# Re-ordering the first sixty microseconds of a cross-attention and quantized feed-forward kernel: weight sums shared anew, first layers moved ahead of side products

## The reference, cut to what matters

```
x = x + cross_attention(layernorm(x), ctx)         # x: 4 x 2048 x 512, ctx: 4 x 154 x 512
x = x + ffn(layernorm(x))

# the mask lets query i see key j only where j % 2048 == i, so that a row
# with i < 154 gets (ctx[i] @ Wv) @ Wout + bout, and every other row the mean of these
def qlinear(x, w, b):
    xq = clip(round(x * sx)), sx = 127 / max|x| of the row
    wq = clip(round(w * sw), -1, 1), sw = 1 / mean|w| of the whole weight
    return (xq @ wq.T) / (sx * sw) + b
h   = layernorm(x) * gamma + beta
h   = gelu(qlinear(h, w1, b1))                       # 512 -> 2048
out = qlinear(h, w2, b2)                             # 2048 -> 512
```

## Time and profile before

| | |
|---|---|
| median of 3 runs | 541.45 us (538.63 to 542.35) |
| the profiled execution | 540.51 us, of which the span is 538.7 us |
| busy in the span | PE 98%, DVE 84%, ACT 81%, POOL 76% |
| the chain of work that ended last | PE 95%, DVE 3%, POOL 1%, ACT 1% |
| stretch from the first to the second weight use (34.15 to 80.81 us) | PE 39.6 of 46.7 us busy, DVE 41.2, ACT 41.1, POOL 37.7 |

### The profile page before, as it was taken

One profiled execution on the slowest core, in us unless ns is written; L12 is line 12 of the kernel. 1 busy time (PEld: TensorE's weight loads), 2 busy tenths in 40 slices (PEclk: granted clock), 3 DMA queues, 4 the chain that ended last, 5 costly groups with the idle time before them and its releaser, 6 DMA issues.

```text
span 538.7 us, 8129 instructions
## 1 busy us (share of the span) xinstructions
PE 527.3 (98%) x2434; PEld 227.4 (42%) x2434; DVE 453.6 (84%) x758; ACT 435.9 (81%) x444; POOL 407.3 (76%) x533
## 2 busy tenths in 40 slices
PE   9979989999999999999999999999999999999997
PEld 5433434444444444444444444444444444444443
DVE  3877999999989899988888887988888889887653
ACT  3558899888887888888888888888888889887762
POOL 2288687999998888888888988888888888873300
PEclk9987999999999999999999999999999999999999
DMA  8999233886565656555665556665455574535433
GB/s 310 402 387 294 69 69 102 170 208 162 135 122 141 131 148 119 129 125 130 131 143 142 123 129 117 141 132 132 124 123 130 129 142 103 92 86 100 95 78 98
DMA packets 137015, 78.72 MB, mean 146 GB/s; under 512 B 114246, under 2 KB 114310, under 8 KB 136972
## 3 DMA queue, kind: packets, MB, share of 16 engines
q1 hardware_dynamic: 135636, 75.80, 57.3%
q10 hardware_dynamic: 1335, 2.41, 1.3%
HBM read 33.88 MB, written 17.05 MB: 95 GB/s over the span
## 4 chain that ended last, share of the span: by engine, by line
PE 95%; DVE 3%; POOL 1%; ACT 1%; issue 1%; POOLq 0%; DVEq 0%; ACTq 0%
PE py L1055 41%; PE p L1040 28%; PE pab L1040 14%; PE p L983 3%; PE p L1030 3%; PE pab L1008 2%; PE pab L1030 1%; POOL xr L387 1%; PE pab L968 1%; DVE hx L792 1%; PE py L1016 1%; PE py L1008 1%; DVE w2q L779 1%; ACT hid L578 0%; PE py L974 0%
## 5 line engine op out<-in xcount | busy, mean ns | idle before, releaser
L1055 PE MATMUL py<-w2q,hqT 128*128 128x512 bf16 x1024 | 231.0, 379 | 1.7 <-DVE hqT L829 1.7
L587 ACT ACTIVATE hq<-hid,hscale 128x2048 int8<-128x2048 f32 x64 | 128.1, 2002 | 46.2 <-DVE hscale L821 46.2
L1040 PE MATMUL p<-w1q,xqT 128*128 128x512 bf16 x688 | 159.4, 380 | 0.0
L1055 PEld LDWEIGHTS py<-w2q,hqT 128*128 128x128 bf16 x1024 | 100.1, 98 | 123.0 <-DVE hqT L829 2.7
L578 ACT ACTIVATE hid<-p,xdeq 128x1024 f32<-128x1024 f32 x86 | 95.0, 1106 | 15.9 <-PE p L1040 11.2
L1040 PEld LDWEIGHTS p<-w1q,xqT 128*128 128x128 bf16 x688 | 63.8, 98 | 81.2 <-issue 10.1
L387 POOL TENSOR_TENSOR xr<-xr,attn 128x512 f32<-128x512 f32 x64 | 83.3, 1320 | 18.7 <-DVE attn L727 17.2
L402 POOL TENSOR_TENSOR hx<-hx,beta_b 128x512 f32<-128x512 f32 x64 | 91.7, 1454 | 4.4 <-ACT hx L563 4.3
L815 DVE TENSOR_REDUCE hmax<-hid 128x1 f32<-128x1025 f32 x64 | 78.1, 1220 | 18.0 <-ACT hid L578 17.4
L406 POOL TENSOR_TENSOR xr<-xr,b_b 128x512 f32<-128x512 f32 x64 | 92.6, 1465 | 0.0
L809 DVE TENSOR_REDUCE hid<-hid 128x1 f32<-128x1024 f32 x64 | 77.4, 1209 | 8.8 <-ACT hid L578 8.8
(11 more groups left out here) (88 smaller groups left out, 408.9 us busy)
## 6 DMA issues: line engine op xcount, KB each, us to landing
xr<-x SPq DMA_DIRECT2D x64, 256.0 KB, 2.9
out<-xr SPq DMA_DIRECT2D x64, 256.0 KB, 2.4
raw<-w1T SPq DMA_DIRECT2D x8, 512.0 KB, 12.2
hid<-wvT SPq DMA_DIRECT2D x8, 256.0 KB, 7.8
wout<-wout_d ACTq DMA_DIRECT2D x8, 256.0 KB, 8.7
wout<-w2T SPq DMA_DIRECT2D x3, 512.0 KB, 5.5
xr<-w2T SPq DMA_DIRECT2D x2, 512.0 KB, 11.1
attn<-ctxm_d SPq DMA_DIRECT2D x4, 256.0 KB, 8.1
```

Source lines behind the costliest of these rows:

```text
L587: nc.scalar.activation(hq8[:, t % 2, :], hid[:, t % 2, 0:HID], ACT.Copy, scale=col(hscale, t))\
L1040: mm = nc.tensor.matmul(hidden_bank(t, n), xT[:, k, :], w1q[:, k, n * D:(n + 1) * D], start=False, stop=(k == KD - 1))
L1055: mm = nc.tensor.matmul(py[:, t % 2, :], hqT[:, t % 2, c // 2, c % 2, :], w2q[:, c, :], start=(c == 0), stop=(c == 2 * NJ - 1))
```

## The change

Five things are changed, all of them in the ramp. (1) The absolute sums: all 8 pieces of w1 are summed by ACT, where DVE had pieces 0 and 4; two pieces of w2 (0 and 1) are summed by DVE, where ACT had all 8. (2) The loads: pieces 0 to 4 of w2 are issued by ACT between its own instructions, where SP issued them; SP's list has x(3) behind w1 and the context ahead of x(4). (3) On PE, `out_rows(2)` stands behind first layer 0, `out_rows(3)` behind first layer 2, and the tail's product behind first layer 3; `weight_total(1)` stands between the halves of first layer 1. (4) `out_rows` waits for the pieces of `wvo` one by one. (5) The orders of ACT, DVE, POOL and SP are written anew around this.

```diff
             def load_w2(j):
-                if j == 3:
-                    sp.wait_ge(mean_done, 1)
                 if j == 5:
                     sp.wait_ge(wvo_done, KD)
...
-            load_x(3)
             load_w1(6)
             load_w1(7)
+            load_x(3)
+            load_ctx()
+            load_b1_rows()
             load_x(4)
-            load_w2(0)
-            load_b1_rows()
...
             transpose_x(0)
             load_w2(5)
             load_w2(6)
+            transpose_x(1)
             load_w2(7)
...
@@ scalar
+            def load_w2(j):
+                if j == 3:
+                    act.wait_ge(mean_done, 1)
+                act.dma_start(w2raw[j], w2T[j * 2 * P:(j + 1) * 2 * P, :].rearrange("(p e) n -> p e n", e=2))\
+                    .then_inc(w2_loaded[j], 16)
...
@@ vector
-            def abs_w1(i):
-                k, h = i // 2, i % 2
-                dve.wait_ge(w1_loaded[i], 16)
-                nc.vector.tensor_reduce(wpart[:, 0, i:i + 1], raw1[:, k, h * HALF:(h + 1) * HALF], AX.X, ALU.add,
+            def abs_w2(n):
+                dve.wait_ge(w2_loaded[n], 16)
+                nc.vector.tensor_reduce(wpart[:, 1, n:n + 1], w2raw[n], AX.XY, ALU.add,
                                         apply_absolute_value=True).then_inc(wabs_dve, 1)
...
@@ tensor
             def out_rows(i):
-                pe.wait_ge(wvo_copied, KD)
...
                 for k in range(KD):
+                    pe.wait_ge(wvo_copied, k + 1)
...
             bias(0)
-            out_rows(2)
             first_layer(0, 0)
             first_layer(0, 1)
-            weight_total(1)
+            out_rows(2)
             bias(1)
             first_layer(1, 0)
+            weight_total(1)
             first_layer(1, 1)
-            out_rows(3)
             bias(2)
             first_layer(2, 0)
             first_layer(2, 1)
-            tail_product()
+            out_rows(3)
             bias(3)
             first_layer(3, 0)
             first_layer(3, 1)
+            tail_product()
             second_layer(0, 0, NJ)
```

More of the change, by code:

```diff
@@ L470, in _ @@
             add_attention(9, 1)
+            inverse_std(6, 2)
             pool.wait_ge(b2_loaded, 16)
             add_b2(0)
-            inverse_std(6, 2)
             add_attention(10, 1)
@@ L658, in _ @@
             round_weights(1, 7)
-            times_std(7)
-            gelu(3, 0)
-            gelu(3, 1)
             round_h(2)
             widen_h(1)
+            times_std(6)
+            times_std(7)
             gelu(4, 0)
+            round_h(3)
+            gelu(4, 1)
             round_x(6)
             round_x(7)
-            gelu(4, 1)
+            widen_h(2)
             times_std(8)
-            widen_h(2)
             times_std(9)
-            round_h(3)
             gelu(5, 0)
@@ L867, in _ @@
             statistics(1)
+            centre(1)
             statistics(2)
[L869 to L871 removed]
             centre(2)
             x_scale(0, 1)
[L874 to L885 removed]
@@ L886, in _ @@
-            attn_rows(0)
-            ctx_sum(3)
-            round_w1(0)
+            weight_sum(0)
+            x_scale(1, 1)
+            weight_scale(0)
+            round_w1(0)
+            clip(0, 0)
+            statistics(3)
+            centre(3)
+            clip(0, 1)
             round_w1(2)
-            clip(0, 0)
-            clip(0, 1)
             clip(0, 2)
             clip(0, 3)
-            attn_rows(1)
+            attn_rows(0)
+            abs_w2(0)
+            abs_w2(1)
@@ L895, in _ @@
+            ctx_sum(0)
+            x_scale(2, 2)
+            ctx_sum(1)
+            attn_rows(1)
+            half_scale(0)
+            ctx_sum(2)
+            statistics(4)
+            hidden_scale(0)
+            centre(4)
+            ctx_sum(3)
+            statistics(5)
+            weight_sum(1)
+            centre(5)
+            weight_scale(1)
             attn_rows(2)
-            weight_sum(1)
+            half_scale(1)
             ctx_means()
-            weight_scale(1)
+            hidden_scale(1)
@@ L899, in _ @@
+            clip(1, 0)
+            clip(1, 1)
+            half_scale(2)
+            hidden_scale(2)
             x_scale(4, 2)
-            half_scale(0)
+            attn_rows(3)
+            clip(1, 2)
+            clip(1, 3)
             statistics(6)
+            half_scale(3)
+            clip(1, 4)
             statistics(7)
-            hidden_scale(0)
-            half_scale(1)
+            hidden_scale(3)
+            clip(1, 5)
+            tail_rows_out()
+            widen_h(0)
+            clip(1, 6)
@@ L905, in _ @@
+            clip(1, 7)
+            widen_h(1)
+            centre(6)
+            centre(7)
             statistics(8)
             statistics(9)
-            hidden_scale(1)
-            centre(6)
-            centre(7)
-            half_scale(2)
-            attn_rows(3)
-            tail_rows_out()
-            hidden_scale(2)
-            clip(1, 0)
-            clip(1, 1)
-            clip(1, 2)
-            clip(1, 3)
-            widen_h(0)
-            clip(1, 4)
-            clip(1, 5)
@@ L921, in _ @@
-            clip(1, 6)
-            clip(1, 7)
-            statistics(10)
-            centre(8)
-            statistics(11)
-            half_scale(3)
-            widen_h(1)
-            x_scale(6, 2)
-            hidden_scale(3)
-            centre(9)
+            x_scale(6, 2)
+            half_scale(4)
+            centre(8)
             result(0)
-            half_scale(4)
             widen_h(2)
             hidden_scale(4)
+            centre(9)
+            statistics(10)
+            statistics(11)
@@ L935, in _ @@
             result(1)
+            half_scale(5)
             centre(10)
+            hidden_scale(5)
+            x_scale(8, 2)
             centre(11)
-            half_scale(5)
-            x_scale(8, 2)
-            hidden_scale(5)
             widen_h(3)
```

127 lines of the change are left out of this document (56 added, 71 removed).

## The result

The changed kernel takes 549.18 us (median of 4 runs, 547.83 to 550.10); the kernel before, run beside it, 540.04 (4 runs, 537.97 to 542.35). The ratio is 1.0166, interval 1.0110 to 1.0222: slower, and outside the forecast range. The profiled execution took 548.3, its span 546.5 against 538.7, so 7.8 us are to be found.

A forecast was written before the change was run, and what follows sets the result against it. PE bounds the kernel, busy 527.3 of 538.7 us, leaving 11 us idle and slow stretches to win. 4.4 us gained at second layer 0 less 2.9 for slow clock is 1.5, against median 541.45: 540.0 us, range 534.8 to 545.5.

The forecast's parts named there:

- the sum's ending at first layer 4: Net gain counted up to first layer 4: 4.4 us at second layer 0 less 2.9 for slow clock, 1.5 us.
- First sum: w1's weight sum: ready before PE ends `products` at 34.15, so `weight_total(0)` no longer waits, slack 0.9 us.
- rival C: Context lands past about 38.5 behind w2 pieces, PE runs dry and the clock falls: 1 to 5 us slower; 15%.
- First layers 0 and 1: First layer 0 starts at 43.9, 7.9 us ahead; PE then waits 2.0 us at `weight_total(1)`, w2's scale ready at 56.3.
- From the scale to second layer 0: ACT's string ends at 75.8, DVE's at 76.4: second layer 0 starts at 76.4, not 80.81, gaining 4.4 us.
- 3.5 + 4.0 = 7.5 us of PE: Price of the first weight sum in the kernel before: 3.5 us idle plus 4.0 us lost to the slow clock.
- Rival A: Clock stays up, or falls harmlessly in the wait at 53.3: 2.8 us gained or more, 537 to 538.7; 25%.
- The new wait for tile 4: Tile 4's transpose lands at 81.6 ahead of first layer 4: hidden behind the slow clock, or costing 1.6 us without it.

The follow-up runs named there:

- the run with both orders mended: Changed kernel with tile 4's work early on GpSimd and DVE's order behind `widen_h(1)` brought back to that of the kernel before: 540.76 us, ratio 1.0007.
- the run with the late statistics: Kernel before with DVE's `statistics(10)` and `statistics(11)` alone moved behind `hidden_scale(4)`: 545.94 us, ratio 1.0138.
- the last run: Kernel before with the early first weight sum, plus DVE's context sums behind `half_scale(0)` and `weight_sum(1)` behind `clip(0, 3)`: 539.49 us, ratio 0.9990.

## Why the prediction was wrong

**The step that failed** is the first: "The change touches no instruction behind tile 6, so all that it can give lies in the 11 us in which PE is idle", and with it the sum's ending at first layer 4, "1.5 or 2.8 us gained". The list of DVE ahead of the loop holds steps of tiles 6 to 11 as well, and the change moves them: DVE's order is changed up to `widen_h(3)`, about 110 us. POOL and ACT have steps that wait for these. PE had no idle time there before, so the prediction took the stretch for out of reach; but no idle time says nothing of slack, that is of how late a step may come before PE has to wait. The list of what would refute it did name the place ("if PE waits in the loop behind tile 6"), with no price and no chance on it. A chance of 0.09 for slower by over 1% was what remained. The runs show the price: about 6.3 us by DVE's order, 2.3 to 3.3 by GpSimd's.

**First sum: right, with less to spare.** `weight_total(0)` starts with no idle ahead, the clock is 1.00, `out_rows` run at 37.16 (forecast 36.8). The sum was ready at 34.0, where 33.3 was forecast; PE came for it at 35.22, not at 34.2, because its 28 entries of `products` began at 23.20 in this execution, not at 21.98. No wait for the context in this execution; so rival C, the slower one that had been priced, is not what happened, though in the profiled execution of the run with both orders mended `out_rows(0)` did wait 2.45 us, until 38.20, and a low stretch of 3.4 us followed. The DMA share stood at 1.06 between 34.0 and 37.1 us, with loads of SP and of ACT under way; it was 1.07 with SP's alone. The rule of the Trainium skill that the prediction weighed ("DMA: Bandwidth & Descriptors", "Issuing engines are not separate DMA queues") agrees with that.

**First layers 0 and 1: nearly right.** Tile 0's transpose, which the prediction had landed in time, held first layer 0 for 0.64 us (44.83, forecast 43.9). The second total waited 1.36 us at 55.74 (forecast 2.0 at 55.3); the second scale was ready at 56.58 (forecast 56.3). DVE's list up to that sum is given as 12.0 us, but its terms add up to 12.55, and it took 12.5 (from 43.0 to 55.45).

**From the scale to second layer 0: DVE's end too short.** ACT's string ended at 76.4 (forecast 75.8). DVE got hidden tile 3 at 73.2 (forecast 72.5), and a clip took 1.31 us there for 0.6 and its half of `widen_h(0)` 1.16, ending at 77.9; forecast 76.4 for second layer 0, measured 78.00, after 5.51 us instead of 4.2. It is 2.8 us before the 80.81 of the earlier trace rows.

**But 80.81 was no fair mark.** The run of before with only `centre(9)` moved is the same program up to there: its first wait is 2.52 us, the clock stays 1.00, and second layer 0 starts at 77.72. In the run with the late statistics the wait is 1.98 us, the clock is low for 3.4 us from 39.3, and second layer 0 starts at 78.99. The profiled execution of before had 3.50 us and 10.2 us at 0.50. So the 4.0 us of slow clock in the price of "3.5 + 4.0 = 7.5 us of PE" come in some executions and not in others. The 52 executions of the kernel before beside the experiments say the same: the 9 with a mean granted clock of 0.991 or less took 541.3 us in the median, the 10 with 0.999 or more took 537.8; the profiled one had 0.990. Moving the first sum alone brought 0.25%, 1.4 us. Rival A's and the forecast's gains both rested on that price. The changed ramp reached second layer 0 at 78.00 here, and at 77.51, 77.98 and 79.44 in three other runs with the same program up to there: against 77.7 to 79.0 it gains nothing that can be seen.

**The new wait for tile 4: right in place, priced too small.** Forecast landing 81.6; PE started at 84.82. `inverse_std(6, 2)` ran at 73.70 (forecast 72.9), two additions took 3.13 for 2.7, the conversion began at 79.01, not at 77.9, and its transpose, issued at 80.28, took 4.5 us to release PE where 2.5 was taken from the earlier trace rows. All of the low clock at second layer 0 hides behind it, as forecast; it cost the 16 entries there 1.7 us (5.36 for 3.63), not 2.9. So first layer 4, which was to start at 82.9 or 81.6, started 1.9 to 3.2 us later than that.

**Rivals.** None was right. A fifth, the rows of DVE that GpSimd and ACT wait for, would have needed a comparison of DVE's order around `widen_h(1)`: `statistics(10)` stood ahead of `widen_h(1)` and now stands behind `hidden_scale(4)`, while POOL's `inverse_std(10, 2)`, which waits for it, kept its place.

**Open.** Why two waits of like length are followed by a low stretch in one execution and not in another isn't settled by these runs.

## What to carry to other kernels

When a change re-orders one engine, compare its whole order up to where the two programs are alike again, and for each step that moved ask which other queue stands at it and what is behind that: a wait in an in-order queue costs what is queued behind, not the waiting step. An engine that is idle nowhere in a stretch has no idle time to win there, but everything to lose. And price a stall from more than one execution where the clock falls in it: here the slow clock behind the same stall cost 4 us in one and nothing in another.

## What the runs showed of the hardware

The granted clock fell at second layer 0 behind a wait of 2.05 us with dense products ahead (0.51 in the 3.5 us from 79.50 to 83.00), and in the last run behind one of 2.53 us (0.57 from 78.00 to 81.00). It stayed at 1.00 behind waits of 2.52 us and 3.44 us in two other kernels. The low stretches were 3.4, 6.8 and 10.2 us long. Behind the longest waits (5.51 and 3.71 us) the clock was low while PE stood still already, from about 74.7 and 102.0 us; that part of the low stretch costs nothing.

The transposes of tiles 4 and 5 let PE go at 84.82, 4.5 us after the first was issued at 80.28, where the earlier trace rows have 2.5 for one. The view of DMA issues of the changed kernel for 80 to 85 us shows them with a hidden tile's transpose beside them:

```profile
xqT<-xq SPq DMA_TRANSPOSE x2, 4.1
hT<-hq SPq DMA_TRANSPOSE x1, 3.5
```
